# Graph attention in two layers: the fourth plain score behind the value matmuls, and three exponentials a step

## Chip, cores, metric

One core of a Trainium2 chip. The metric is device microseconds of one execution of the program, the median of several runs.

## What is computed

Two layers of masked multi-head attention on 4096 rows of 128 features, each followed by a feed-forward block. Cut to its core:

```python
qkv = layer_norm(x, g1, be1) @ w_qkv            # 8 heads of 16
scores = jnp.einsum('nhd,mhd->hnm', q, k) * SCALE
scores = jnp.where((adj != 0)[None], scores, -jnp.inf)
attn = jax.nn.softmax(scores, axis=-1)
out = jnp.einsum('hnm,mhd->nhd', attn, v).reshape(n, DIM)
x = x + out @ w_proj + b_proj
h2 = layer_norm(x, g2, be2)
x = x + jax.nn.gelu(h2 @ w1 + b1) @ w2 + b2
```

## The kernel before

A layer has three phases with barriers between them: the projections (`project`), the attention (`attend`), and the output projection with the feed-forward block. The change touches the attention alone, which takes most of the time.

The attention computes each score twice. Once plainly, with queries on the partitions (`score_a`, called A here), so that VectorE can take the masked maximum of each row (`take_max`, L802). And once transposed, with keys on the partitions and the maxima already subtracted by two more rows of the operands (`score_b`, called B), so that ScalarE's exponential of it (`exp_pair`, L667) can go straight into the value matmul (`gather_v`, L459, called V). There are 16 passes a layer (8 blocks of 512 queries, 4 heads at a time) of 32 steps, one for each tile of 128 keys; 512 steps a layer. The plain scores run ahead of the others by a pass and 20 scores (`FIRST`, 148): each step issues four of the plain scores for a later pass, A0 to A3, and the last 37 steps have none left.

Plain scores have three PSUM banks, used in turn: a score waits for the take of the one three before it (`a_done`). The B scores of a step have four banks, one a head, written again in each step as soon as their exponentials are done (`b_exped`). V has one bank that sums over the 32 steps of a pass. A take of A0 opens a new tile of the row mask and so waits for that tile as well as for the score; those of A1 to A3 wait for their score alone.

TensorE's matmuls for A, B and the masks have 48, 50 or 64 rows and stand in one half of the array's rows each, so that two neighbours on different halves can run at once (`r0` is 0 or 64). The four value matmuls use all rows and 32 columns each. The mask of the B scores is added on TensorE, as an identity matmul of bf16 in two halves (`add_mask`, L472, called m): for heads 0 and 1 in every step, and for heads 2 and 3 only in steps that are not `pooled`, which are the even steps in the even passes of layer 0 (called full-mask steps). In all others GpSimd multiplies the exponentials of heads 2 and 3 by a 0/1 mask (`mask_pair`, L950), in place, ahead of V. The second half of a bank's mask waits until the first halves of that pair are done (`half_added`), since both halves of the array write to one bank then.

V of a step is issued two steps later (`LAG`). `p_buf`, where the exponentials go, has four slots. ScalarE also makes row masks (L684), in about every other pass of layer 0, and keeps V's sums once a pass (L675). SyncE issues all DMAs of the phase in an order sorted by step numbers. At the end of a pass the maxima go to DRAM and come back as two rows of the query operand (`max_dram`, `q_ready`), for which the first B0 of a pass waits. Each engine otherwise follows the order in which its code is written.

In a step the order on TensorE is A0 A1, B0 B1, m m, B2 B3, m m, A2 A3, V; a full-mask step has two more pairs of m, around A2 A3. B0 waits for the first exponential of the step before, B2 for the second.

Of the kernel before, what the change touches and what calls it, by code (L numbers as in the profile page):

```python
# [57 lines left out]
def scores_before(t):  # L58
    return min(FIRST + 4 * t, NSC)
# [12 lines left out]
def gnn_kernel(nc, x, adj, adj_t, weights, signs, ident, ident_f, out):  # L72
    ctx = ExitStack()
    with ctx:
# [3 lines left out]
        def sem(name):  # L78
            return ctx.enter_context(nc.semaphore(name))
# [82 lines left out]
        max_ready, hi_ready, hi_kept, neg_ready = sem("max_ready"), sem("hi_ready"), sem("hi_kept"), sem("neg_ready")  # L162
        turned, max_stored, q_ready = sem("turned"), sem("max_stored"), sem("q_ready")
        half_added = sem("half_added")
        b_scored, b_exped, pv_done, o_kept = sem("b_scored"), sem("b_exped"), sem("pv_done"), sem("o_kept")
        o_stored = [sem("o_stored_0"), sem("o_stored_1")]

        o_loaded, o_turned, attn_ready = sem("o_loaded"), sem("o_turned"), sem("attn_ready")
# [44 lines left out]
        def masked_before(L, t):  # L213
            return sum(POOLED[l][STEPS] for l in range(L)) + POOLED[L][t]
# [14 lines left out]
        def _(sp):  # L229
# [51 lines left out]
            def load_added(L, i):  # L281
                nb, s = i // MT, i % MT
                if i >= 4:
                    sp.wait_ge(mt_loaded[i % 4], i // 4 * 16)
                if nb > 0:
                    sp.wait_ge(b_scored, L * 2 * STEPS + 2 * ((nb - 1) * 2 * MT + MT + s) + 2)
                sp.dma_start(mask_t[:, s, :], mt_dram[i]).then_inc(mt_loaded[i % 4], 16)

            def load_q(L, nb):
                if nb >= Q_SLOTS:  # L290
                    sp.wait_ge(b_scored, L * 2 * STEPS + (nb - Q_SLOTS + 1) * 4 * MT)
                slot = (L * NB + nb) % Q_SLOTS
                sp.dma_start(q_t[:, slot].rearrange("p i c -> p (i c)").bitcast(F32),
                             q_dram[nb].rearrange("p i c -> p (i c)")).then_inc(q_loaded[slot], 16)
# [108 lines left out]
        def _(pe):  # L403
# [43 lines left out]

            def gather_v(L, t):
                quad, s = t // MT % 2, t % MT
                pe.wait_ge(b_exped, L * 2 * STEPS + 2 * t + 2)  # L450
                if pooled(L, t):
                    pe.wait_ge(p_masked, masked_before(L, t + 1))
                if s == 0:
                    done = L * 2 * NB + t // MT
                    if done > 0:
                        pe.wait_ge(o_kept, done)
                for j in range(4):
                    h = 4 * quad + j
                    mm = pe.matmul(ps_o[32 * j:32 * j + 32, :], v_sb[:, (s * HEADS + h) * VW:(s * HEADS + h) * VW + 32],  # L459
                                   p_buf[:, t % P_SLOTS, j, :], start=s == 0, stop=s == MT - 1, skip_group_check=True)  # L460
                mm.then_inc(pv_done, 1)
# [13 lines left out]
            def b_step(L, t):  # L475


                nb, quad, s = t // (2 * MT), t // MT % 2, t % MT
                jobs = range(scores_before(t), scores_before(t + 1))
                for j in jobs[:2]:  # L480
                    score_a(L, j)
                if L == 0:
                    pe.wait_ge(t_made, nb * MT + s + 1)
                else:
                    pe.wait_ge(mt_loaded[s % 4], (nb * MT + s) // 4 * 16 + 16)
                if t > 0:
                    pe.wait_ge(b_exped, L * 2 * STEPS + 2 * t - 1)
                if s == 0:
                    pe.wait_ge(q_ready, (L * PASSES + t // MT + 1) * 64)
                score_b(L, t, 0), score_b(L, t, 1)  # L490
                if len(jobs) >= 4:
                    add_mask(s, 0, 0), add_mask(s, 1, 1).then_inc(half_added, 1)
                    added[0] += 1
                    if t > 0:
                        pe.wait_ge(b_exped, L * 2 * STEPS + 2 * t)
                    score_b(L, t, 2), score_b(L, t, 3)
                    pe.wait_ge(half_added, added[0])
                    if pooled(L, t):
                        add_mask(s, 1, 0), add_mask(s, 0, 1).then_inc(b_scored, 2)
                        for j in jobs[2:]:  # L500
                            score_a(L, j)
                    else:
                        add_mask(s, 1, 0), add_mask(s, 0, 1).then_inc(b_scored, 1)
                        add_mask(s, 2, 0), add_mask(s, 3, 1).then_inc(half_added, 1)
                        added[0] += 1
                        for j in jobs[2:]:
                            score_a(L, j)
                        pe.wait_ge(half_added, added[0])
                        add_mask(s, 3, 0), add_mask(s, 2, 1).then_inc(b_scored, 1)
                else:  # L510
                    for j in range(2):
                        mm = pe.matmul(ps_b[:, j, :], idb[:], mask_t[:, s, :], start=False, stop=True)
                    mm.then_inc(b_scored, 1)
                    for j in jobs[2:]:
                        score_a(L, j)
                    if t > 0:
                        pe.wait_ge(b_exped, L * 2 * STEPS + 2 * t)
                    score_b(L, t, 2)
                    mm = score_b(L, t, 3)
                    if not pooled(L, t):  # L520
                        for j in range(2, 4):
                            mm = pe.matmul(ps_b[:, j, :], idb[:], mask_t[:, s, :], start=False, stop=True)
                    mm.then_inc(b_scored, 1)
                if t >= LAG:
                    gather_v(L, t - LAG)

            def attend(L):
                for n in range(FIRST):
                    score_a(L, n)
                for t in range(STEPS):  # L530
                    b_step(L, t)
                for t in range(STEPS - LAG, STEPS):
                    gather_v(L, t)
# [86 lines left out]
        def _(act):  # L620
# [38 lines left out]
                    round_qk(gi)  # L659
                    keep_v(gi, g)  # L660

            def exp_pair(L, t, half):
                k = L * 2 * STEPS + 2 * t + half
                act.wait_ge(b_scored, k + 1)
                if half == 0 and t >= P_SLOTS:
                    act.wait_ge(pv_done, L * STEPS + t - P_SLOTS + 1)
                nc.scalar.activation(p_buf[:, t % P_SLOTS, 2 * half:2 * half + 2, :], ps_b[:, 2 * half:2 * half + 2, :],  # L667
                                     ACT.Exp, scale=SCALE).then_inc(b_exped, 1)

            def keep_o(L, i):  # L670
                gi = L * 2 * NB + i
# [15 lines left out]
            def attend(L):  # L687
                visits = [v for v in range(NV) if rows_made(L, v)]
                made = 0
                while made < len(visits) and visit_step(visits[made]) < 3:  # L690
                    mask_rows(visits[made])
                    made += 1
                for t in range(STEPS):
                    if t > LAG and t % MT == LAG:
                        keep_o(L, t // MT - 1)
                    exp_pair(L, t, 0)
                    exp_pair(L, t, 1)
                    while made < len(visits) and visit_step(visits[made]) - 3 < t + 1:
                        mask_rows(visits[made])
                        made += 1  # L700
                keep_o(L, 2 * NB - 1)
# [214 lines left out]
        def _(pool):  # L916
# [13 lines left out]
            def make_masks(t):  # L930
                nb, s, slot = t // (2 * MT), t % MT, t % M_SLOTS
                m = mask01[:, slot, :]
                pool.wait_ge(adjt_loaded[slot], fills(0, t) * 16)
                pool.tensor_scalar(m, m.bitcast(U32), 1.0, 0.0, ALU.min, ALU.max).then_inc(mask01_made, 1)  # L934
                if nb > 0:
                    pool.wait_ge(b_scored, 2 * (t - MT) + 2)
                    if s == 0:
                        pool.wait_ge(mt_stored, nb * MT * 16)
                pool.wait_ge(mask01_made, MADE[t + 1])
                pool.tensor_scalar(mask_t[:, s, :], m, -MASKED, MASKED, ALU.mult, ALU.add).then_inc(t_made, 1)  # L940

            def mask_pair(L, t):
                pool.wait_ge(b_exped, L * 2 * STEPS + 2 * t + 2)
                if made(L, t):
                    pool.wait_ge(mask01_made, MADE[t + 1])
                else:
                    pool.wait_ge(adjt_loaded[t % M_SLOTS], fills(L, t) * 16)  # L947
                p = p_buf[:, t % P_SLOTS, 2:4, :].bitcast(I32)
                m = mask01[:, t % M_SLOTS, :].rearrange("p (a c) -> p a c", a=1).broadcast_to([P, 2, TILE])
                pool.tensor_tensor(p, p, m, ALU.mult).then_inc(p_masked, 1)  # L950
# [70 lines left out]
```

## Time and profile before

| what | value |
|---|---|
| median of 3 runs | 3551.73 us (3551.18 to 3558.91) |
| the profiled execution | 3553.85 us, span 3552.1 us |
| TensorE busy | 3402.5 us, 96% |
| VectorE busy | 2847.8 us, 80% |
| GpSimd busy | 2482.2 us, 70% |
| ScalarE busy | 2334.7 us, 66% |

Shares are of the span. The attention of layer 0 lies from about 207 to 1685 us, that of layer 1 from about 1998 to 3437 us. The times of VectorE, GpSimd and ScalarE are those of their instructions; a matmul's end is modelled, and its time contains the flight through the array.

### The profile page before, as it was taken

Reading aid. Unit: us, or ns where it says so; the run is one execution under the profiler, and the core shown is the slowest. Engines: PE = TensorE matmul, PEld = TensorE weight load, DVE = VectorE, ACT = ScalarE, POOL = GpSimd, SP = SyncE. Lnnn points to the kernel's source line nnn. Section 1 sums busy time; section 2 is a strip of 40 time slices with the busy share of each in tenths; the row PEclk is TensorE's granted clock in tenths of the full one; section 3 lists DMA queues with packets and bytes.
Section 4 is the critical chain, followed back from the end, with each engine's and each line's share of the span. In section 5 each row is a group of like instructions: output and inputs, shape, how many; then the busy total and the mean of one; then the engine's idle time right before and its main releaser. Section 6 shows DMA issues by size and latency. Waiting matters only on the chain.

```text
span 3552.1 us, 68184 instructions
## 1 busy us (share of the span) xinstructions
PE 3402.5 (96%) x22292; PEld 1415.3 (40%) x22312; DVE 2847.8 (80%) x8964; ACT 2334.7 (66%) x2596; POOL 2482.2 (70%) x1476
## 2 busy tenths in 40 slices
PE   5999999999999999999768999999999999999988
PEld 3443333333333333332544433333333333333326
DVE  6898888888888888880458898999989999989604
ACT  4348777777778787868342366666666666666753
POOL 1057878787878788789110388888888888888870
PEclk9689999999999999999887699999999999999989
DMA  4578787878786978774222455555555555555432
GB/s 134 175 225 264 240 272 233 283 230 293 220 285 216 297 222 293 231 254 118 90 92 102 136 169 175 172 173 171 175 172 171 176 168 179 166 179 167 148 92 69
DMA packets 487006, 677.34 MB, mean 191 GB/s; under 512 B 57952, under 2 KB 279264, under 8 KB 482272
## 3 DMA queue, kind: packets, MB, share of 16 engines
q1 hardware_dynamic: 486224, 672.88, 60.7%
q8 instruction: 182, 2.98, 0.3%
q14 instruction: 168, 1.38, 0.1%
q10 hardware_dynamic: 432, 0.10, 0.0%
HBM read 508.67 MB, written 166.20 MB: 190 GB/s over the span
## 4 chain that ended last, share of the span: by engine, by line
PE 44%; POOL 38%; issue 11%; DMA 2%; ACT 1%; POOLq 1%; DVE 1%; SPq 1%; DVEq 0%; ACTq 0%
POOL arena L950 38%; PE PS L445 15%; PE PS L459 12%; PE PS L472 7%; PE PS L466 6%; PE PS L421 3%; POOLq L928 1%; DMA q_t<-max_dram 1%; ACT arena L667 1%; DVE arena L762 0%; PE PS L582 0%; PE PS L412 0%; SPq L303 0%; POOL arena L940 0%; POOLq L947 0%
## 5 line engine op out<-in xcount | busy, mean ns | idle before, releaser
L802 DVE CUSTOM_DVE_ANT_0 spill<-PS,mask_n 128x512 bf16<-128x512 f32 x4096 | 2594.9, 688 | 323.7 <-PE PS L445 315.1
L667 ACT ACTIVATE arena<-PS 128x1024 f32<-128x1024 f32 x2048 | 1986.4, 1022 | 812.0 <-PE PS L472 777.7
L950 POOL TENSOR_TENSOR arena<-arena,mask 128x1024 int32<-128x1024 int32 x896 | 2130.7, 2378 | 547.5 <-ACT arena L667 542.6
L445 PE MATMUL PS<-k_t,q_t 48*128 48x512 f32 x4096 | 1407.9, 539 | 15.9 <-DMA q_t<-q_dram 12.0
L459 PE MATMUL PS<-arena,v_sb 128*32 128x512 f32 x8192 | 1095.1, 607 | 6.4 <-POOL arena L950 5.6
L445 PEld LDWEIGHTS PS<-k_t,q_t 48*128 48x128 f32 x4096 | 619.6, 195 | 1049.0 <-DVE pmax L802 932.3
L466 PE MATMUL PS<-q_t,k_t 50*128 50x512 f32 x4096 | 909.6, 478 | 9.8 <-DMA q_t<-max_dram 9.0
L472 PE MATMUL PS<-arena,idb 64*128 64x512 bf16 x4304 | 836.0, 390 | 0.0
L466 PEld LDWEIGHTS PS<-q_t,k_t 50*128 50x128 f32 x4096 | 396.5, 187 | 109.9 <-issue 73.5
L472 PEld LDWEIGHTS PS<-arena,idb 64*128 64x128 bf16 x4304 | 208.3, 95 | 475.4 <-issue 291.2
L802 DVE DVE_READ_ACCUMULATOR2_ANT pmax<- 128x1 f32 x4096 | 344.6, 84 | 0.0
L459 PEld LDWEIGHTS PS<-arena,v_sb 128*32 128x32 f32 x8192 | 161.9, 108 | 260.5 <-issue 257.3
L934 POOL TENSOR_SCALAR mask<-mask 128x512 int32<-128x512 uint32 x256 | 157.2, 614 | 140.4 <-DMA mask<-in_adj_t 131.9
L923 POOL TENSOR_SCALAR arena<-arena 128x4 f32<-128x4 f32 x32 | 7.3, 228 | 322.4 <-DVE arena L753 322.4
L684 ACT ACTIVATE mask_n<-adj_in,far 128x512 bf16<-128x512 uint32 x256 | 184.8, 723 | 44.1 <-DVE pmax L802 31.0
L940 POOL TENSOR_SCALAR arena<-mask 128x512 bf16<-128x512 int32 x256 | 158.1, 618 | 37.5 <-POOL mask L934 34.3
L868 DVE RECIPROCAL arena<-PS 128x32 f32<-128x32 f32 x16 | 5.7, 357 | 206.2 <-PE PS L543 205.4
L421 PE MATMUL PS<-arena,wts 128*128 128x512 f32 x256 | 114.5, 601 | 0.0
L713 ACT ACTIVATE arena<-PS,wts 128x512 f32<-128x512 f32 x64 | 43.9, 687 | 52.6 <-PE PS L572 50.9
L629 ACT ACTIVATE arena<-PS,wts 128x512 f32<-128x512 f32 x32 | 24.9, 777 | 77.4 <-PE PS L412 45.6
L412 PE MATMUL PS<-idf,arena 128*128 128x128 f32 x64 | 12.3, 323 | 63.7 <-DVE arena L762 63.7
L421 PEld LDWEIGHTS PS<-arena,wts 128*128 128x128 f32 x256 | 48.5, 195 | 54.6 <-issue 54.6
(51 smaller groups left out, 841.7 us busy)
## 6 DMA issues: line engine op xcount, KB each, us to landing
mask<-m_dram SPq DMA_DIRECT2D x768, 256.0 KB, 2.8
mask_n<-mn_dram SPq DMA_DIRECT2D x768, 128.0 KB, 2.8
adj_in<-in_adj SPq DMA_DIRECT2D x256, 256.0 KB, 4.2
mask<-in_adj_t SPq DMA_DIRECT2D x256, 256.0 KB, 4.2
m_dram<-mask SPq DMA_DIRECT2D x256, 256.0 KB, 3.7
mn_dram<-mask_n SPq DMA_DIRECT2D x256, 128.0 KB, 4.3
mt_dram<-arena SPq DMA_DIRECT2D x256, 128.0 KB, 3.5
arena<-mt_dram SPq DMA_DIRECT2D x256, 128.0 KB, 2.9
```

Source lines behind the costliest of these rows:

```text
L421: pe.matmul(PS[:, 2 + i % 4, :], wts[:, C_QK + i * P:C_QK + (i + 1) * P], xn_t[:, gx % 2, :], start=True, stop=True).then_inc(qk_ready, 1)
L445: pe.matmul(ps_a[:, (L * NSC + n) % A_BANKS, :], q_t[r0:r0 + KROWS, gb % Q_SLOTS, pair, q * P:(q + 1) * P], k_t[r0:r0 + KROWS, pair, mb * ...
L459: mm = pe.matmul(ps_o[32 * j:32 * j + 32, :], v_sb[:, (s * HEADS + h) * VW:(s * HEADS + h) * VW + 32], p_buf[:, t % P_SLOTS, j, :], start= ...
L466: return pe.matmul(ps_b[:, j, :], k_t[r0:r0 + BROWS, pair, s * P:(s + 1) * P], q_t[r0:r0 + BROWS, (L * NB + nb) % Q_SLOTS, pair, :], start ...
L472: return pe.matmul(ps_b[:, j, :], idb[r0:r0 + 64, :], mask_t[r0:r0 + 64, s, :], start=False, stop=part != j % 2)
L667: nc.scalar.activation(p_buf[:, t % P_SLOTS, 2 * half:2 * half + 2, :], ps_b[:, 2 * half:2 * half + 2, :], ACT.Exp, scale=SCALE).then_inc( ...
L684: nc.scalar.activation(mask_n[:, slot, :], adj_in[:, m % ADJ_SLOTS, :].bitcast(U32), ACT.Exp, bias=far[:], scale=MASKED).then_inc(n_made, 1)
L713: nc.scalar.activation(g_t[:, f, :], PS[:, 4 + f, :], ACT.Gelu_apprx_tanh, bias=wts[:, C_B1 + f:C_B1 + f + 1]).then_inc(gelu_done, 1)
L802: dve.tensor_tensor_reduce(spill[:, bank, :], ps_a[:, bank, :], mask_n[:, v % N_SLOTS, :], 1.0, LOWEST, ALU.subtract, ALU.max, pmax[:, p % ...
L934: pool.tensor_scalar(m, m.bitcast(U32), 1.0, 0.0, ALU.min, ALU.max).then_inc(mask01_made, 1)
L940: pool.tensor_scalar(mask_t[:, s, :], m, -MASKED, MASKED, ALU.mult, ALU.add).then_inc(t_made, 1)
L950: pool.tensor_tensor(p, p, m, ALU.mult).then_inc(p_masked, 1)
```

## The change

On TensorE, A3 of a step is issued after V, beside A0 of the next step. A1 moves next to B2, B3 next to a mask piece, and A2 next to the last mask piece of the first pair. A common step is A3' A0, B0 B1, m m, B2 A1, m B3, A2 m, V, where A3' is the one carried over. A full-mask step is A3' A0, B0 B1, m m, B2 A1, m B3, m m, A2 m, m m, V.

On ScalarE the exponentials of heads 2 and 3, one instruction of 1024 columns before, are two of 512, each with its own semaphore in both directions (`scored`, `exped`). In common steps with plain scores head 2 goes first, then heads 0 and 1, then head 3; in all others heads 0 and 1 go first. B2 waits for the exponential of head 2, B3 for that of head 3. GpSimd waits for both. VectorE, SyncE and the DMAs keep their instructions and order; they wait for the new semaphores where they waited for the old ones.

```diff
             def b_step(L, t):
...
-                jobs = range(scores_before(t), scores_before(t + 1))
-                for j in jobs[:2]:
-                    score_a(L, j)
+                n, last = scores_before(t), scores_before(t + 1)
+                done = L * STEPS + t
+                if n > scores_before(t - 1):
+                    score_a(L, n - 1)
+                if last > n:
+                    score_a(L, n)
...
+                if t > 0:
+                    pe.wait_ge(exped[0], done)
                 score_b(L, t, 0), score_b(L, t, 1)
-                if len(jobs) >= 4:
+                if last > n:
                     add_mask(s, 0, 0), add_mask(s, 1, 1).then_inc(half_added, 1)
                     added[0] += 1
                     if t > 0:
-                        pe.wait_ge(b_exped, L * 2 * STEPS + 2 * t)
-                    score_b(L, t, 2), score_b(L, t, 3)
+                        pe.wait_ge(exped[1], done)
+                    mm = score_b(L, t, 2)
+                    if pooled(L, t):
+                        mm.then_inc(scored[1], 1)
+                    score_a(L, n + 1)
                     pe.wait_ge(half_added, added[0])
+                    add_mask(s, 1, 0)
+                    if t > 0:
+                        pe.wait_ge(exped[2], done)
+                    mm = score_b(L, t, 3)
                     if pooled(L, t):
-                        add_mask(s, 1, 0), add_mask(s, 0, 1).then_inc(b_scored, 2)
-                        for j in jobs[2:]:
-                            score_a(L, j)
+                        mm.then_inc(scored[2], 1)
+                        score_a(L, n + 2), add_mask(s, 0, 1).then_inc(scored[0], 1)
                     else:
-                        add_mask(s, 1, 0), add_mask(s, 0, 1).then_inc(b_scored, 1)
                         add_mask(s, 2, 0), add_mask(s, 3, 1).then_inc(half_added, 1)
                         added[0] += 1
-                        for j in jobs[2:]:
-                            score_a(L, j)
+                        score_a(L, n + 2), add_mask(s, 0, 1).then_inc(scored[0], 1)
                         pe.wait_ge(half_added, added[0])
-                        add_mask(s, 3, 0), add_mask(s, 2, 1).then_inc(b_scored, 1)
+                        add_mask(s, 3, 0).then_inc(scored[2], 1), add_mask(s, 2, 1).then_inc(scored[1], 1)
...
-            def exp_pair(L, t, half):
-                k = L * 2 * STEPS + 2 * t + half
-                act.wait_ge(b_scored, k + 1)
-                if half == 0 and t >= P_SLOTS:
+            def exp_heads(L, t, part):
+                act.wait_ge(scored[part], L * STEPS + t + 1)
+                if t >= P_SLOTS:
                     act.wait_ge(pv_done, L * STEPS + t - P_SLOTS + 1)
-                nc.scalar.activation(p_buf[:, t % P_SLOTS, 2 * half:2 * half + 2, :], ps_b[:, 2 * half:2 * half + 2, :],
-                                     ACT.Exp, scale=SCALE).then_inc(b_exped, 1)
+                heads = (slice(0, 2), slice(2, 3), slice(3, 4))[part]
+                nc.scalar.activation(p_buf[:, t % P_SLOTS, heads, :], ps_b[:, heads, :],
+                                     ACT.Exp, scale=SCALE).then_inc(exped[part], 1)
...
-                    exp_pair(L, t, 0)
-                    exp_pair(L, t, 1)
+                    for part in (1, 0, 2) if pooled(L, t) and scores_before(t + 1) > scores_before(t) else (0, 1, 2):
+                        exp_heads(L, t, part)
```

TensorE in a common step of layer 1, before: L459 is V, L445 a plain score, L466 a B score, L472 a half mask. The rows run from one V to the next.

```order
L459 MATMUL PS<-arena,v_sb 32x512 [waits p_masked,b_exped]
L459 MATMUL PS<-arena,v_sb 32x512 x3
L445 MATMUL PS<-k_t,q_t 128x512 [waits a_done] x2
L466 MATMUL PS<-q_t,k_t 128x512 [waits b_exped,mt_loaded_3]
L466 MATMUL PS<-q_t,k_t 128x512
L472 MATMUL PS<-arena,idb 128x512 x2
L466 MATMUL PS<-q_t,k_t 128x512 [waits b_exped]
L466 MATMUL PS<-q_t,k_t 128x512
L472 MATMUL PS<-arena,idb 128x512 [waits half_added]
L472 MATMUL PS<-arena,idb 128x512
L445 MATMUL PS<-k_t,q_t 128x512 [waits a_done] x2
```

The same step after the change: L466 is V there, L449 a plain score, L473 a B score, L479 a half mask.

```order
L466 MATMUL PS<-arena,v_sb 32x512 [waits p_masked,exped_01]
L466 MATMUL PS<-arena,v_sb 32x512 x3
L449 MATMUL PS<-k_t,q_t 128x512 [waits a_done] x2
L473 MATMUL PS<-q_t,k_t 128x512 [waits exped_01,mt_loaded_3]
L473 MATMUL PS<-q_t,k_t 128x512
L479 MATMUL PS<-arena,idb 128x512 x2
L473 MATMUL PS<-q_t,k_t 128x512 [waits exped_2]
L449 MATMUL PS<-k_t,q_t 128x512 [waits a_done]
L479 MATMUL PS<-arena,idb 128x512 [waits half_added]
L473 MATMUL PS<-q_t,k_t 128x512 [waits exped_3]
L449 MATMUL PS<-k_t,q_t 128x512 [waits a_done]
L479 MATMUL PS<-arena,idb 128x512
```

Two plain scores stand behind V in both, but they are A3' and A0 now; ahead of V a plain score and the last mask piece, which releases the first exponential pair, take the place of A2 A3.

ScalarE in common steps of layer 1, before (L667 is the exponential):

```order
L667 ACTIVATE arena<-PS 128x1024 [waits pv_done,b_scored]
L667 ACTIVATE arena<-PS 128x1024 [waits b_scored]
L667 ACTIVATE arena<-PS 128x1024 [waits pv_done,b_scored]
L667 ACTIVATE arena<-PS 128x1024 [waits b_scored]
L667 ACTIVATE arena<-PS 128x1024 [waits pv_done,b_scored]
```

And after (L682 is the exponential; `scored_2` stands for head 2, `scored_01` for heads 0 and 1):

```order
L682 ACTIVATE arena<-PS 128x512 [waits pv_done,scored_2]
L682 ACTIVATE arena<-PS 128x1024 [waits pv_done,scored_01]
L682 ACTIVATE arena<-PS 128x512 [waits pv_done,scored_3]
L682 ACTIVATE arena<-PS 128x512 [waits pv_done,scored_2]
L682 ACTIVATE arena<-PS 128x1024 [waits pv_done,scored_01]
```

One of two instructions a step became two of half its size, and one of these now stands ahead of the pair of heads 0 and 1.

## Rows read from the trace of the kernel before

**Rows 1.** The page: span, busy time of each engine, chain that ended last.

```profile
span 3552.1 us, 68184 instructions
PE 3402.5 (96%) x22292; PEld 1415.3 (40%) x22312; DVE 2847.8 (80%) x8964; ACT 2334.7 (66%) x2596; POOL 2482.2 (70%) x1476
...
PE 44%; POOL 38%; issue 11%; DMA 2%; ACT 1%; POOLq 1%; DVE 1%; SPq 1%; DVEq 0%; ACTq 0%
```

**Rows 2.** Windows, 100 us of layer 1: busy by engine, PEclk, DMA share, GB/s.

```profile
2500.00:2600.00 100.00, 100.00 (x712) 39.45 (x709) 90.32 (x290) 69.28 (x72) 84.36 (x36) 1.00 0.64 192
```

**Rows 3.** Timeline, layer 1: start, length in us, engine, line, operation, [idle before].

```profile
2499.33 0.69 DVE L802 CUSTOM_DVE_ANT_0 spill<-PS,mask_n 128x512 bf16<-128x512 f32 x1 [0.29 <-PE PS L445]
...
2499.72 0.39 PE L472 MATMUL PS<-arena,idb 64*128 64x512 bf16 x2
...
2500.09 0.18 PEld L445 LDWEIGHTS PS<-k_t,q_t 48*128 48x128 f32 x1 [0.17 <-DVE pmax L802]
2500.15 1.94 ACT L667 ACTIVATE arena<-PS 128x1024 f32<-128x1024 f32 x2 [0.86 <-PE PS L472]
...
2500.52 1.06 PE L459 MATMUL PS<-arena,v_sb 128*32 128x512 f32 x8
...
2501.51 0.50 PE L445 MATMUL PS<-k_t,q_t 48*128 48x512 f32 x2
...
2501.86 0.40 PE L466 MATMUL PS<-q_t,k_t 50*128 50x512 f32 x2
...
2502.09 0.39 PE L472 MATMUL PS<-arena,idb 64*128 64x512 bf16 x2
...
2502.14 0.58 PE L466 MATMUL PS<-q_t,k_t 50*128 50x512 f32 x2
2502.16 0.69 DVE L802 CUSTOM_DVE_ANT_0 spill<-PS,mask_n 128x512 bf16<-128x512 f32 x1 [0.29 <-PE PS L445]
2502.17 2.38 POOL L950 TENSOR_TENSOR arena<-arena,mask 128x1024 int32<-128x1024 int32 x1 [0.42 <-ACT arena L667]
...
2502.57 0.39 PE L472 MATMUL PS<-arena,idb 64*128 64x512 bf16 x2
```

**Rows 4.** Waits in the same 100 us: total, times, longest.

```profile
PEld PS L445 <- DVE pmax L802: 31.2, 46, 0.8
```

**Rows 5.** Timeline of a full-mask step in layer 0.

```profile
1001.82 0.50 PE L445 MATMUL PS<-k_t,q_t 48*128 48x512 f32 x2
...
1002.86 0.61 PE L472 MATMUL PS<-arena,idb 64*128 64x512 bf16 x4
...
1003.55 0.39 PE L472 MATMUL PS<-arena,idb 64*128 64x512 bf16 x2
...
1003.74 0.69 DVE L802 CUSTOM_DVE_ANT_0 spill<-PS,mask_n 128x512 bf16<-128x512 f32 x1
...
1003.87 1.07 PE L459 MATMUL PS<-arena,v_sb 128*32 128x512 f32 x8
...
1004.87 0.50 PE L445 MATMUL PS<-k_t,q_t 48*128 48x512 f32 x2
```

**Rows 6.** The same step, a window that ends ahead of A3.

```profile
1003.12 0.58 PE L445 MATMUL PS<-k_t,q_t 48*128 48x512 f32 x1
```

**Rows 7.** Groups of instructions on ScalarE: busy us, mean ns, idle before.

```profile
L667 ACT ACTIVATE arena<-PS 128x1024 f32<-128x1024 f32 x2048 | 1986.4, 1022 | 812.0 <-PE PS L472 777.7 <-PE PS L512 34.2
L684 ACT ACTIVATE mask_n<-adj_in,far 128x512 bf16<-128x512 uint32 x256 | 184.8, 723 | 44.1 <-DVE pmax L802 31.0 <-DMA adj_in<-in_adj 13.2
...
L675 ACT COPY o_sb<-PS 128x512 f32<-128x512 f32 x32 | 18.9, 591 | 8.3 <-PE PS L459 8.3
```

**Rows 8.** The page's groups: the half-mask matmuls.

```profile
L472 PE MATMUL PS<-arena,idb 64*128 64x512 bf16 x4304 | 836.0, 390 | 0.0
```

**Rows 9.** Timeline of TensorE behind a pass edge in layer 0.

```profile
301.89 0.50 PE L466 MATMUL PS<-q_t,k_t 50*128 50x512 f32 x2 [1.59 <-DMA q_t<-max_dram]
...
302.69 0.41 PE L472 MATMUL PS<-arena,idb 64*128 64x512 bf16 x2
```

**Rows 10.** Timeline in the last steps of layer 0, without plain scores.

```profile
1619.98 7.17 POOL L950 TENSOR_TENSOR arena<-arena,mask 128x1024 int32<-128x1024 int32 x3
```

More of the change, by code:

```diff
@@ L164, in gnn_kernel @@
         half_added = sem("half_added")
-        b_scored, b_exped, pv_done, o_kept = sem("b_scored"), sem("b_exped"), sem("pv_done"), sem("o_kept")
+        scored = [sem("scored_01"), sem("scored_2"), sem("scored_3")]
+        exped = [sem("exped_01"), sem("exped_2"), sem("exped_3")]
+        pv_done, o_kept = sem("pv_done"), sem("o_kept")
         o_stored = [sem("o_stored_0"), sem("o_stored_1")]
@@ L285, in load_added @@
                 if nb > 0:
-                    sp.wait_ge(b_scored, L * 2 * STEPS + 2 * ((nb - 1) * 2 * MT + MT + s) + 2)
+                    sp.wait_ge(scored[0], L * STEPS + (nb - 1) * 2 * MT + MT + s + 1)
                 sp.dma_start(mask_t[:, s, :], mt_dram[i]).then_inc(mt_loaded[i % 4], 16)
@@ L290, in load_q @@
                 if nb >= Q_SLOTS:
-                    sp.wait_ge(b_scored, L * 2 * STEPS + (nb - Q_SLOTS + 1) * 4 * MT)
+                    for part in range(3):
+                        sp.wait_ge(scored[part], L * STEPS + (nb - Q_SLOTS + 1) * 2 * MT)
                 slot = (L * NB + nb) % Q_SLOTS
@@ L449, in gather_v @@
                 quad, s = t // MT % 2, t % MT
-                pe.wait_ge(b_exped, L * 2 * STEPS + 2 * t + 2)
+                pe.wait_ge(exped[0], L * STEPS + t + 1)
                 if pooled(L, t):
                     pe.wait_ge(p_masked, masked_before(L, t + 1))
+                else:
+                    pe.wait_ge(exped[1], L * STEPS + t + 1)
+                    pe.wait_ge(exped[2], L * STEPS + t + 1)
                 if s == 0:
@@ L485, in b_step @@
                     pe.wait_ge(mt_loaded[s % 4], (nb * MT + s) // 4 * 16 + 16)
-                if t > 0:
-                    pe.wait_ge(b_exped, L * 2 * STEPS + 2 * t - 1)
                 if s == 0:
                     pe.wait_ge(q_ready, (L * PASSES + t // MT + 1) * 64)
+                if t > 0:
+                    pe.wait_ge(exped[0], done)
                 score_b(L, t, 0), score_b(L, t, 1)
-                if len(jobs) >= 4:
+                if last > n:
                     add_mask(s, 0, 0), add_mask(s, 1, 1).then_inc(half_added, 1)
@@ L512, in b_step @@
                         mm = pe.matmul(ps_b[:, j, :], idb[:], mask_t[:, s, :], start=False, stop=True)
-                    mm.then_inc(b_scored, 1)
-                    for j in jobs[2:]:
-                        score_a(L, j)
+                    mm.then_inc(scored[0], 1)
                     if t > 0:
[L517 to L520, printed above, removed]
+                        pe.wait_ge(exped[1], done)
+                        pe.wait_ge(exped[2], done)
+                    if pooled(L, t):
+                        score_b(L, t, 2).then_inc(scored[1], 1), score_b(L, t, 3).then_inc(scored[2], 1)
+                    else:
+                        score_b(L, t, 2), score_b(L, t, 3)
                         for j in range(2, 4):
                             mm = pe.matmul(ps_b[:, j, :], idb[:], mask_t[:, s, :], start=False, stop=True)
-                    mm.then_inc(b_scored, 1)
+                            mm.then_inc(scored[j - 1], 1)
                 if t >= LAG:
@@ L527, in attend @@
             def attend(L):
-                for n in range(FIRST):
+                for n in range(0, FIRST - 1):
                     score_a(L, n)
@@ L935, in make_masks @@
                 if nb > 0:
-                    pool.wait_ge(b_scored, 2 * (t - MT) + 2)
+                    pool.wait_ge(scored[0], t - MT + 1)
                     if s == 0:
@@ L942, in mask_pair @@
             def mask_pair(L, t):
-                pool.wait_ge(b_exped, L * 2 * STEPS + 2 * t + 2)
+                pool.wait_ge(exped[1], L * STEPS + t + 1)
+                pool.wait_ge(exped[2], L * STEPS + t + 1)
                 if made(L, t):
```

## The prediction

> **What bounds the kernel now.** The page first: TensorE is busy 96% of a span of 3552.1 us, VectorE 80%, GpSimd 70%, ScalarE 66%, and the chain that ended last runs through PE and POOL [rows 1]. A 96% that contains waits with a matmul still in flight decides nothing, so I read one stretch of layer 1, where every step is alike: the granted clock is 1.00 there (2.4 GHz), and 36 mask products in 100 us make a step some 2.8 us [rows 2]. Then the timeline of one step [rows 3], to see which waits repeat. Call the four plain scores of a step A0 to A3, the four scores for the softmax B0 to B3, the half-mask matmuls m, and the four value matmuls V. VectorE starts its take of A0 at 2499.33 and again at 2502.16: a step is 2.83 us. Follow it round:
> - A0 and A1 start at 2501.51; A0 takes 0.50 and ends at 2502.01; VectorE starts on it at 2502.16. That is 0.65 us, and VectorE had been idle for 0.29 before it.
> - Three banks hold plain scores, so A3 needs A0's bank. From VectorE's start at 2499.33 to the weight load of A3 at 2500.09, whose wait the row puts down to that engine: 0.76.
> - A3 to V: 2500.09 to 2500.52, 0.43. V to the next A0: 2500.52 to 2501.51, 0.99 (the stretch 0.995 that repeats).
>
> 0.65 + 0.76 + 0.43 + 0.99 = 2.83. **This loop through the three banks is the bound** of such a step. The grouped waits agree: the weight loads of plain scores are the ones on PE that wait for VectorE, 31.2 us in 100, most of it while V runs [rows 4]. A second loop is just as long by eye: m ends at 2500.11, the two exponentials run from 2500.15 for 1.94 to 2502.09, and B2 starts at 2502.14. But m had started only at 2502.09 and its 0.21 of columns was under way, so B2 lost little by it.
>
> A step that adds all its masks on PE (every second one in the even passes of layer 0) goes from A0 at 1001.82 to A0 at 1004.87, 3.05 us [rows 5]. Its A3 does not hold up V, since two more mask slots follow; the matmuls themselves bound it. In the last 37 steps of a layer, without plain scores, three mask products follow each other in 7.17 us: 2.39 a step, GpSimd's own rate [rows 10].
>
> **How many of each.** Each layer has 475 steps with plain scores. 4304 half-mask matmuls [rows 8] = 4 x 950 + 4 x 126, so 126 of the 950 are such full-mask steps and 824 are not.
>
> **The change part by part.**
>
> *The number of matmuls and slots* stays: six pairs and V in a common step, eight pairs and V in a full-mask step. A3 of a step now starts after V, beside the next A0; A2 is the last one ahead of V. A2 needs the bank of that A3. So the loop has the same four members: first score behind V, its take, last score ahead of V, V. Carrying the score over does not by itself lengthen the distance, and I give it nothing.
>
> *What it does change in the loop* is which take comes first behind V. Before, it is that of A0, the one that opens a new mask tile and waits for two semaphores, the tile's and the score's. Its start lies 0.15 behind the matmul's end (2502.01 to 2502.16, rows 3). A take that waits for one is to be seen in the full-mask step: A2 starts at 1003.12 and takes 0.58 [rows 6], so it ends at 1003.70, and VectorE, idle by then, starts at 1003.74 [rows 5], 0.04 later. After the change the first take behind V is A3's, with one wait; A0's second wait falls behind a take that is still running. Worth 0.11 us: 0.54 + 0.76 + 0.43 + 0.99 = **2.72**. Bounds of this term: 0 (the delay belongs to the spot behind V, not to the waits) and 0.11.
>
> *Split exponentials.* Two of 1024 columns a step become one of 1024 and two of 512. One of 1024 takes 1.02; a copy of 512 out of PSUM takes 0.59, the exponential of 512 from SBUF 0.72 [rows 7]. Two in a row start 0.92 apart (1.94 less 1.02). I take 0.59 and 0.49 for the distance, by the copy, since it reads the same memory; the upper end is 0.62. ScalarE's load goes from 1.84 to 0.92 + 2 x 0.49 = 1.90, with the row masks of the odd passes 2.53: under 2.72, so free, and 2.8 at the upper ends. What matters is the order. The first pair's last mask piece now stands behind A2's wait, and its exponential is needed by B0, the second slot behind V. That loop: B0 to the mask piece that waits for half_added, 301.89 to 302.69, 0.80 [rows 9]; B3, issued behind that wait, shows its weight load, 0.10 (a score behind V takes 0.50, one whose load is hidden 0.40, rows 3); one slot 0.24 (2501.86 to 2502.09); the last piece 0.39; to ScalarE 0.04; 1.02; to B0 0.05, or 0.16 since B0 waits for two semaphores. Sum **2.64 to 2.75**. This is what is late next, within 0.03 of the other loop on either side. I take 2.72 to 2.73 for a common step, a gain of **0.10**: 824 x 0.10 = -82 us. Bounds: -91 (0.11) and -41 (0.05).
>
> B2's wait for both exponentials goes: it now needs the one that was done first. As said, it cost little. GpSimd needs the last exponential, which ends some 1.6 behind V instead of 1.57; its 2.38 still fits in 2.72, and V takes its product two steps later.
>
> *Full-mask steps.* B3 stands behind the half_added wait with an unhidden f32 load, 0.10, where a bf16 piece stood, whose load costs next to nothing. The piece behind it on its row half, m31, is late by this, the pair that waits for it too (1002.86 to 1003.55 to 1003.87 in rows 5), and nothing here has slack. +0.10 x 126 = **+13 us**; bounds 0 and +20.
>
> *Pass edges.* The maxima of a pass are complete about half a microsecond later (the last take stands behind V), and the softmax scores of the first step wait for them by way of DMA: 1.59 once [rows 9]. The extra reductions also meet less idle time on VectorE. 30 edges at 0.1: **+3**; bounds 0 and +10.
>
> *The tail* (37 steps a layer) stays at GpSimd's 2.39: its scores and exponentials keep their order, and 1.90 of ScalarE fits. SP's queue and all DMAs are the same; they are issued by steps, so they only come 3% closer together.
>
> **Sum.** -82 + 13 + 3 = -66. The profiled execution took 3553.9 us, so 3488; the median of the runs stands 2.1 lower, 3551.7, so **3486 us**.
>
> **Rivals.**
> 1. *The exponential's loop takes over (slower).* The first pair's scores are signalled behind A2's wait, and everything down to B0 is in series. If the 512-column exponentials follow at 0.62, the first one (head 2) delays the 1024 one by some 0.05, and with B0's double wait 0.05 dearer than my 0.16 the loop is 2.75 + 0.10 = 2.85. From 2.81 on it eats the whole gain. 824 x 0.03 + 13 + 3 = +41: some **3592**, and 3550 where it only equals the old bound. For it: the two loops are within 0.03 already. Against: every piece but two has its own row. Chance 0.14.
> 2. *Nothing in the loop moves.* The 0.15 belongs to waking VectorE behind V. Then 2.83 stays and the full-mask steps pay: 3552 + 16 = **3568**. Against it are the rows of the one-wait take. Chance 0.07.
> 3. *Unlike pairs do not overlap.* All pairs in the trace are of one type. PE's own time for a common step, with no wait, is 0.99 (V) + 0.34 (A to B) + 0.24 (B to m) + 0.48 (m to m, rows 3) + 0.24 + 0.32 (m to V, rows 5) = 2.61. If an f32 score and a bf16 mask piece run one after the other, two slots of 512 columns at 2.4 GHz come on top, 0.43: 3.04, or 0.21 more than 2.83; a full-mask step gets 0.43 + 0.11: 824 x 0.21 + 126 x 0.54 = +241, **3793**. For it: nothing shows such a pair. Against: the halves have separate rows, loads and banks. Chance 0.09.
> 4. *Semaphore updates.* A common step has nine matmuls that update one, before it had seven, and each is a little work at PE's end. No row isolates it; the nearest is that A to B takes 0.34 behind two updates and B to m 0.24 behind none, so up to 0.05 each: 2.72 + 0.10 at most, 2.77 in the middle, **3530**. Chance 0.05. The Trainium skill ("TensorE: Matmul & The Clock Gate", Part 3, the cost per tile) says that increments of packed matmuls serialise at 26.3 ns each; by that figure the sum would be some 43 us higher, an estimate, and no row here confirms it.
>
> The forecast's own mechanism has 0.65, with 3461 to 3531 by its bounds.
>
> **Range and chances.** 3455 to 3568 takes in the forecast (0.65), rival 4 (0.05), rival 2 (0.07) and the milder part of rival 1 (0.06). A measurement tells about 0.2% (7 us) from no change. Faster 0.74, same 0.07, slower 0.19.
>
> **What would show it.** In layer 1, V to V at 2.71 to 2.75; VectorE's first take behind V 0.04 behind the matmul's end; its idle time before a take down from 0.29 to about 0.2. The full-mask steps at 3.15. ScalarE's 512-column exponentials at 0.59. The forecast is wrong if PE's waits name ScalarE at B0 for most steps (rival 1), if the first take still starts 0.15 late (rival 2), or if the slot with B3 and a mask piece takes 0.45 instead of 0.24 (rival 3).

## The result, and the profile after

| | before | after |
|---|---|---|
| median | 3553.03 us (4 runs, 3551.18 to 3558.91) | 3503.24 us (4 runs, 3495.38 to 3505.25) |
| profiled execution | 3553.85, span 3552.1 | 3504.94, span 3503.2 |

The ratio is 0.9853, with a 95% interval of 0.9833 to 0.9873: **1.5% faster**, 50 us, where 3486 had been forecast.

The page after, to be read beside [rows 1]. TensorE's share is the same 96%, ScalarE has gained 145 us of work, and the chain that ended last has left GpSimd (38% of it before, 1% now).

```profile
span 3503.2 us, 71453 instructions
PE 3351.8 (96%) x22292; PEld 1483.3 (42%) x22312; DVE 2840.6 (81%) x8964; ACT 2479.3 (71%) x3620; POOL 2484.2 (71%) x1476
...
PE 80%; issue 5%; DVE 3%; DMA 2%; POOL 1%; SPq 1%; ACT 1%; POOLq 1%; DVEq 0%; ACTq 0%
```

Where the time went is best read from the distance between the first value matmuls of successive steps, taken from both traces:

| steps (how many) | median, before | median, after | sum, before | sum, after | change |
|---|---|---|---|---|---|
| layer 1, common (472) | 2.820 | 2.734 | 1336.7 | 1294.5 | -42.1 |
| layer 0, odd passes (224) | 2.820 | 2.734 | 650.2 | 630.8 | -19.4 |
| layer 0, even passes, common (124) | 2.820 | 2.712 | 351.7 | 340.3 | -11.4 |
| layer 0, full-mask (124) | 3.050 | 3.212 | 380.2 | 397.9 | +17.7 |
| last steps of both layers (78) | 2.39 | 2.39 | 186.8 | 187.5 | +0.7 |
| all that lies ahead, between and behind | | | 646.6 | 652.1 | +5.6 |

The sum of the changes, -48.9, is the difference of the spans. The last row is nearly all code that the change doesn't touch. It varies between the traces of this study as well, from 646.1 to 652.5 (646.9 in experiment 1 below and 651.8 in experiment 4, both without a carried score), and its cause stays open.

A common step of layer 1 after the change. L449 is a plain score, L473 a B score, L479 a half mask, L466 V. A piece mjk is the half mask of head j on half k of the array's rows: m10 waits for half_added and m01 is the last one of the first pair. These rows answer to [rows 3]; start and length are in us.

```profile
2499.93 0.21 PEld L473 LDWEIGHTS PS<-q_t,k_t 50*128 50x128 f32 x2
...
2500.20 0.69 DVE L817 CUSTOM_DVE_ANT_0 spill<-PS,mask_n 128x512 bf16<-128x512 f32 x1 [0.19 <-PE PS L449]
...
2500.28 0.41 PE L479 MATMUL PS<-arena,idb 64*128 64x512 bf16 x2
...
2500.76 0.39 PE L479 MATMUL PS<-arena,idb 64*128 64x512 bf16 x1
2500.77 0.49 PE L473 MATMUL PS<-q_t,k_t 50*128 50x512 f32 x1
...
2500.93 2.11 ACT L682 ACTIVATE arena<-PS 128x512 f32<-128x512 f32 x3 [0.63 <-PE PS L473]
2500.95 0.18 PEld L449 LDWEIGHTS PS<-k_t,q_t 48*128 48x128 f32 x1
...
2501.11 0.39 PE L479 MATMUL PS<-arena,idb 64*128 64x512 bf16 x1
...
2501.42 1.06 PE L466 MATMUL PS<-arena,v_sb 128*32 128x512 f32 x8
...
2501.53 1.02 ACT L682 ACTIVATE arena<-PS 128x1024 f32<-128x1024 f32 x1
...
2502.42 0.50 PE L449 MATMUL PS<-k_t,q_t 48*128 48x512 f32 x2
...
2502.67 0.21 PEld L473 LDWEIGHTS PS<-q_t,k_t 50*128 50x128 f32 x2
2502.75 0.45 PE L473 MATMUL PS<-q_t,k_t 50*128 50x512 f32 x2
2502.95 0.69 DVE L817 CUSTOM_DVE_ANT_0 spill<-PS,mask_n 128x512 bf16<-128x512 f32 x1 [0.22 <-PE PS L449]
```

(The row at 2500.93 merges the three exponentials of a step; the one at 2501.53 is the middle one, of heads 0 and 1, from a narrower view. The row at 2499.93, B0's and B1's weight loads, is from a narrower view too.)

The first scores behind V end at 2502.92 and VectorE starts at 2502.95, 0.03 later; before it was 0.15. The rest of the loop through the banks: take to A2's weight load 0.75 (2500.20 to 2500.95), A2 to V 0.47, V to the next scores 1.00. Note the 0.47, which was 0.43: V now waits for the mask piece at 2501.11, not for A2. I put that piece's lateness down to B3's weight load, which stands in the open at 2500.76 behind the wait for half_added: it is 0.34 from B3 to the piece that follows on the same half of the array. Experiment 6 tests this. B0 and B1 are late as well: the exponential of heads 0 and 1 ended at 2502.55 and their weight loads start at 2502.67, 0.25 behind A's start where it was 0.11 (2501.62 in the trace before). The masks behind them come 0.59 to 0.62 behind A, before 0.58.

The loop through that exponential can be followed in these rows from one weight load of B0 (2499.93) to the next (2502.67): 0.83 to m10, 0.35 to m01, 0.39 for it, 0.04 to ScalarE, 1.02 for the exponential, 0.11 to B0's load. That is 2.73 to 2.74, the median step.

A full-mask step after, to be read beside [rows 5]:

```profile
788.35 0.50 PE L449 MATMUL PS<-k_t,q_t 48*128 48x512 f32 x2
...
788.97 0.41 PE L479 MATMUL PS<-arena,idb 64*128 64x512 bf16 x2
...
789.45 0.39 PE L479 MATMUL PS<-arena,idb 64*128 64x512 bf16 x1
789.46 0.49 PE L473 MATMUL PS<-q_t,k_t 50*128 50x512 f32 x1
789.67 0.38 PE L479 MATMUL PS<-arena,idb 64*128 64x512 bf16 x1
...
789.80 0.84 PE L479 MATMUL PS<-arena,idb 64*128 64x512 bf16 x4
```

From B3's pair to the piece m31 on B3's half it is 789.45 to 789.80, 0.35; before, the two pairs of pieces at this place followed each other at 0.23. And the first masks stand 0.62 behind A. Two delays, then, where I had counted one.

### The profile page after: what moved, and what is told of

The parts are those of the page before. It is cut to its first block, busy times and chain, and to the rows that moved or that the text cites. A ratio compares the mean times of both kernels' runs of the same rounds, so it can differ in the third digit from the quotient of the medians.

```text
span 3503.2 us, 71453 instructions
## 1 busy us (share of the span) xinstructions
PE 3351.8 (96%) x22292; PEld 1483.3 (42%) x22312; DVE 2840.6 (81%) x8964; ACT 2479.3 (71%) x3620; POOL 2484.2 (71%) x1476
## 4 chain that ended last, share of the span: by engine, by line
PE 80%; issue 5%; DVE 3%; DMA 2%; POOL 1%; SPq 1%; ACT 1%; POOLq 1%; DVEq 0%; ACTq 0%
PE PS L466 28%; PE PS L449 18%; PE PS L473 16%; PE PS L479 14%; DVE spill L817 2%; PE PS L425 2%; PE PS L527 1%; POOL arena L966 1%; ACT arena L682 1%; DMA q_t<-max_dram 1%; POOLq L943 1%; PE PS L597 0%; DMA max_dram<-stage_t 0%; SPq L307 0%; DVE arena L777 0%
## 5 line engine op out<-in xcount | busy, mean ns | idle before, releaser
L682 ACT ACTIVATE arena<-PS 128x512 f32<-128x512 f32 (+1 forms) x3072 | 2133.3, 739 | 615.3 <-PE PS L473 371.6
L449 PE MATMUL PS<-k_t,q_t 48*128 48x512 f32 x4096 | 1694.2, 542 | 14.2 <-DMA q_t<-q_dram 12.1
L473 PE MATMUL PS<-q_t,k_t 50*128 50x512 f32 x4096 | 1258.1, 485 | 11.8 <-DMA q_t<-max_dram 9.0
L479 PE MATMUL PS<-arena,idb 64*128 64x512 bf16 x4304 | 1150.5, 389 | 0.0
L466 PE MATMUL PS<-arena,v_sb 128*32 128x512 f32 x8192 | 1094.8, 606 | 8.2 <-POOL arena L966 7.9
L449 PEld LDWEIGHTS PS<-k_t,q_t 48*128 48x128 f32 x4096 | 627.3, 195 | 942.4 <-DVE pmax L817 898.6
L473 PEld LDWEIGHTS PS<-q_t,k_t 50*128 50x128 f32 x4096 | 594.5, 188 | 209.1 <-issue 112.1
L479 PEld LDWEIGHTS PS<-arena,idb 64*128 64x128 bf16 x4304 | 310.4, 94 | 376.5 <-PE PS L479 230.7
L466 PEld LDWEIGHTS PS<-arena,v_sb 128*32 128x32 f32 x8192 | 161.7, 108 | 248.2 <-issue 248.2
```

What stands on the lines that cost most here:

```text
L449: pe.matmul(ps_a[:, (L * NSC + n) % A_BANKS, :], q_t[r0:r0 + KROWS, gb % Q_SLOTS, pair, q * P:(q + 1) * P], k_t[r0:r0 + KROWS, pair, mb * ...
L473: return pe.matmul(ps_b[:, j, :], k_t[r0:r0 + BROWS, pair, s * P:(s + 1) * P], q_t[r0:r0 + BROWS, (L * NB + nb) % Q_SLOTS, pair, :], start ...
L479: return pe.matmul(ps_b[:, j, :], idb[r0:r0 + 64, :], mask_t[r0:r0 + 64, s, :], start=False, stop=part != j % 2)
L682: nc.scalar.activation(p_buf[:, t % P_SLOTS, heads, :], ps_b[:, heads, :], ACT.Exp, scale=SCALE).then_inc(exped[part], 1)
```

## The experiments

All kernels below compute the whole result. Lengths of a common step are medians in layer 1, from V to V. The kernel before was run again beside each group: 3551.7 us beside the first four, 3554.7 beside the second four, and the ratios are to these.

**1. The kernel before, with one wait moved.** The row-mask tile of the next four takes is waited for at A3's take.

```diff
-                if i == 0:
-                    if rows_made(L, v):
-                        dve.wait_ge(n_made, ROWS_MADE[v + 1])
+                if n == 0 or (i == 3 and v + 1 < NV):
+                    u = v if n == 0 else v + 1
+                    if rows_made(L, u):
+                        dve.wait_ge(n_made, ROWS_MADE[u + 1])
                     else:
-                        dve.wait_ge(mn_loaded[v % N_SLOTS], rows_loads(L, v) * 16)
+                        dve.wait_ge(mn_loaded[u % N_SLOTS], rows_loads(L, u) * 16)
```

> The kernel before, with one edit on VectorE: the wait for the next row-mask tile stands at the take of A3 (which finds a backlog) and no longer at the take of A0, so the first take behind V waits for the score alone. Order and waits of TensorE, ScalarE and GpSimd are those of before. Theory (the double wait of the first take behind V costs 0.11 us in the loop through the three banks): a common step goes from 2.82 to between 2.71 and 2.76, the latter where the loop through both exponentials takes over (0.39 + 0.04 + 1.94 + 0.05 + 0.34 = 2.76); 824 steps x 0.06 to 0.11 = 50 to 90 us, so 3463 to 3503 beside 3553. Full-mask steps stay at 3.05. Rival (the delay belongs to the place behind V): 3553, and VectorE still starts 0.15 behind the matmul's end.

Measured: 3506.93 us, ratio 0.9872 (0.9858 to 0.9887). A common step takes 2.770, in the even passes of layer 0 2.712, a full-mask step 3.10. The timeline of layer 1:

```profile
2540.11 1.94 ACT L667 ACTIVATE arena<-PS 128x1024 f32<-128x1024 f32 x2 [0.83 <-PE PS L472]
...
2541.22 0.50 PE L445 MATMUL PS<-k_t,q_t 48*128 48x512 f32 x2
...
2541.76 0.69 DVE L803 CUSTOM_DVE_ANT_0 spill<-PS,mask_n 128x512 bf16<-128x512 f32 x1
...
2542.11 0.19 PEld L466 LDWEIGHTS PS<-q_t,k_t 50*128 50x128 f32 x2 [0.22 <-ACT arena L667]
```

A0 ends at 2541.72 and VectorE starts at 2541.76. The wait, not the place, was the 0.11. And the next bound shows at once: B2's load waits for ScalarE now, which [rows 3] had shown without cost. So one moved wait on VectorE brings nearly as much as the whole change (45 us against 50). It stops at 2.77 because both exponentials lie in a loop of that length, 0.39 + 0.04 + 1.94 + 0.05 + 0.34 = 2.76. The full-mask steps did not stay at 3.05 as I had expected: B2's load waits for the exponentials of the step before there as well (608.65 to 608.70 in layer 0 of its trace).

**2. The changed kernel, with the same edit.** There it puts two waits on the first take behind V.

> The changed kernel with the same edit on VectorE: the wait for the next row-mask tile moves to the take of A3, which is there the first one behind V, so that one has two waits again. Theory: its start goes from 0.04 to 0.15 behind the matmul's end and a common step from 2.73 to 2.84; 824 x 0.11 = +90, some 3590; about 3560 to 3600, slower than before, since the full-mask steps keep their 3.21. Rival (the place decides): 3503, no change.

Measured: 3566.86 us, ratio 1.0037 (1.0023 to 1.0052): slower than before. A common step is back at 2.820, and the full-mask steps keep 3.211.

```profile
2540.69 0.49 PE L449 MATMUL PS<-k_t,q_t 48*128 48x512 f32 x2
...
2541.33 0.69 DVE L818 CUSTOM_DVE_ANT_0 spill<-PS,mask_n 128x512 bf16<-128x512 f32 x1 [0.28 <-PE PS L449]
```

2541.18 to 2541.33 is the 0.15 again. The step is 2.82 and not the 2.84 I expected, since with VectorE late the last mask piece no longer holds up V. With experiment 1 this shows the cause of the gain from both sides: the change without its side effect on the waits costs 15 us.

**3. The split exponentials alone**, with TensorE's order of before.

```diff
-                    exp_pair(L, t, 0)
-                    exp_pair(L, t, 1)
+                    for part in (0, 1, 2):
+                        exp_heads(L, t, part)
```

(with B2 waiting for `exped[1]`, B3 for `exped[2]`, and the scores signalled apart, as in the change)

> TensorE's order of before (A2 and A3 ahead of V), with the changed kernel's three exponentials a step and their separate semaphores, heads 0 and 1 first, then head 2, then head 3. B2 waits for the exponential of head 2, B3 for that of head 3. Theory: the loop through the banks stays at 2.82 and the full-mask steps at 3.05, so nothing moves: 3553 within 7 us. Rival (the exponentials' loop was the real bound, and the split is what brought the gain): a common step at 2.73 or below, 3480 or below.

Measured: 3551.33 us, ratio 1.0000 (0.9990 to 1.0009), a common step of 2.820. As expected, but the next run shows that it proves less than I thought.

**4. The split, and the moved wait of experiment 1.**

> As the run with the split alone, and in addition the wait for the next row-mask tile at the take of A3, so that the first take behind V (A0) waits for one semaphore. No score is carried over V. Theory: both loops are relieved, the one through the banks is at 2.71 to 2.72 and the one through the exponentials well below; full-mask steps stay at 3.05: 3553 - 824 x 0.105 = 3466 (3460 to 3475), so faster than the changed kernel by some 35 us. If the carried score is needed for the gain, this one stays near 3553; if pairing unlike matmuls brings something of its own, it stays above 3503.

Measured: 3548.72 us, ratio 0.9991 (0.9981 to 1.0000). **Wrong by 83 us**: with the split on top of experiment 1 its gain is gone. The trace says why:

```profile
2540.26 2.00 ACT L682 ACTIVATE arena<-PS 128x1024 f32<-128x1024 f32 x3 [0.82 <-PE PS L479]
...
2542.32 0.18 PEld L473 LDWEIGHTS PS<-q_t,k_t 50*128 50x128 f32 x1 [0.16 <-ACT arena L682]
...
2542.41 0.09 PEld L479 LDWEIGHTS PS<-arena,idb 64*128 64x128 bf16 x1
...
2542.66 0.39 PE L479 MATMUL PS<-arena,idb 64*128 64x512 bf16 x1
...
2543.09 1.02 ACT L682 ACTIVATE arena<-PS 128x1024 f32<-128x1024 f32 x1 [0.82 <-PE PS L479]
```

Three exponentials in a row take 2.00, the pair took 1.94. B3 waits for the last of them, loads its weights in the open, and the mask piece on its half (2542.66) releases the next three. From 2540.26 to 2543.09 the loop is 2.83. This loop was there in experiment 3 as well (2.82 in its trace), next to the banks' loop of the same length, so that run could not tell them apart.

**5. The same, with head 2 first.**

```diff
-                    for part in (0, 1, 2):
+                    for part in (1, 0, 2) if pooled(L, t) and scores_before(t + 1) > scores_before(t) else (0, 1, 2):
```

> TensorE's order of before, three exponentials a step, the first take behind V with one wait, as the run that stayed at 3549, but with head 2's exponential ahead of that of heads 0 and 1, as in the changed kernel. Theory: in that run the loop m01, three exponentials in a row, B3 took over (0.39 + 0.04 + 0.92 + 0.48 + 0.60 + 0.05 + 0.34 = 2.82); with head 2 first only two of them lie in the loop and the banks' 2.71 is the bound again, full-mask steps near 3.05: 3553 - 824 x 0.105 = 3466 (3460 to 3480), faster than the changed kernel, without a carried score. If it stays near 3549, the cause of that run was another one (the number of waits on B2 and B3, or the unhidden load of B3 by itself).

Measured: **3464.62 us**, ratio 0.9748 (0.9728 to 0.9768). A common step takes 2.712, a full-mask step 3.043. The timeline of layer 1 on ScalarE, which works on head 2 while the last mask pieces are still being added:

```profile
2539.76 2.00 ACT L682 ACTIVATE arena<-PS 128x512 f32<-128x512 f32 x3 [0.71 <-PE PS L473]
2542.47 1.51 ACT L682 ACTIVATE arena<-PS 128x512 f32<-128x512 f32 x2 [0.70 <-PE PS L473]
```

Order alone is worth 84 us here. This kernel has the change's exponentials and the single wait, but carries no score over V, and it beats the changed kernel by 39 us. Summed as in the table above, its trace is 42.6 us shorter: 19 lie in the full-mask steps, which the carried order lengthens, 17 in the common steps of all passes, and 6 in the last row, which has no cause here.

**6. The changed kernel, with B3 ahead of the wait for half_added.**

```diff
-                    pe.wait_ge(half_added, added[0])
-                    add_mask(s, 1, 0)
                     if t > 0:
                         pe.wait_ge(exped[2], done)
                     mm = score_b(L, t, 3)
+                    pe.wait_ge(half_added, added[0])
+                    add_mask(s, 1, 0)
```

> The changed kernel with B3 issued ahead of the wait for half_added and of the mask piece m10, so that its weight load runs beside the plain score A1. Theory (the unhidden load of B3 costs 0.10 in the full-mask steps and lies in the loop through heads 0 and 1's exponential): full-mask steps from 3.21 to 3.11, common steps of whole passes from 2.735 to the banks' 2.71: 126 x 0.10 + 698 x 0.02 = -27, so 3476 (3470 to 3485). Rival (unlike pairs run one after the other, and that is where the 0.10 is): full-mask steps stay at 3.21, 3503.

Measured: 3474.17 us, ratio 0.9769 (0.9752 to 0.9787). Common steps 2.700, full-mask steps 3.130.

```profile
2542.26 0.39 PE L479 MATMUL PS<-arena,idb 64*128 64x512 bf16 x1
2542.27 0.39 PE L473 MATMUL PS<-q_t,k_t 50*128 50x512 f32 x1
2542.43 0.49 PE L449 MATMUL PS<-k_t,q_t 48*128 48x512 f32 x1
2542.50 0.39 PE L479 MATMUL PS<-arena,idb 64*128 64x512 bf16 x1
```

B3 and the mask piece start together, and the next piece on B3's half follows 0.23 later, the same as for a pair of one type. So the unlike matmuls do overlap, and the delay between B3 and the next piece was B3's weight load.

**7. The changed kernel, with heads 2 and 3 in one exponential again.**

```diff
+                if part == 1:
+                    act.wait_ge(scored[2], L * STEPS + t + 1)
...
-                heads = (slice(0, 2), slice(2, 3), slice(3, 4))[part]
+                heads = (slice(0, 2), slice(2, 4))[part]
...
-                    for part in (1, 0, 2) if pooled(L, t) and scores_before(t + 1) > scores_before(t) else (0, 1, 2):
+                    for part in (0, 1):
```

(B3 waits for the same exponential as B2)

> The changed kernel with the exponentials of heads 2 and 3 in one instruction of 1024 columns again, behind that of heads 0 and 1, as before. The carried score and TensorE's order stay. Theory (the score carried over V puts the last mask piece late, so the exponentials must be split and reordered for it to pay): the loop m01, two exponentials, B2, m10, B3, m01 takes 0.39 + 0.04 + 1.94 + 0.05 + 0.34 + 0.34 = 3.1 in a common step: 3553 + 824 x 0.28 + 20 = some 3800 (3750 to 3850). Rival (the split is free dressing): 3503.

Measured: 3725.28 us, ratio 1.0478 (1.0462 to 1.0495), a common step of 3.026. With heads 2 and 3 in one exponential behind that of heads 0 and 1, the carried score loses 222 us against the changed kernel. This edit takes back the split and the order together; one exponential of heads 2 and 3 ahead of that of heads 0 and 1 was not run, so it stays open which of the two the carried score needs. I had the loop 0.07 too long: half_added has long been reached when B2's wait ends, so B3's weight load is hidden.

```profile
2542.70 0.50 PE L474 MATMUL PS<-q_t,k_t 50*128 50x512 f32 x1
...
2543.04 0.39 PE L480 MATMUL PS<-arena,idb 64*128 64x512 bf16 x1
2543.05 0.40 PE L474 MATMUL PS<-q_t,k_t 50*128 50x512 f32 x1
...
2543.29 0.39 PE L480 MATMUL PS<-arena,idb 64*128 64x512 bf16 x1
```

B2 to m10 is 0.34, m10 to the last piece 0.25.

**8. The changed kernel, with one wait on B0.** The wait for the mask tile moves to the score behind V.

```diff
+                if L == 0:
+                    pe.wait_ge(t_made, nb * MT + s + 1)
+                else:
+                    pe.wait_ge(mt_loaded[s % 4], (nb * MT + s) // 4 * 16 + 16)
                 if n > scores_before(t - 1):
                     score_a(L, n - 1)
```

(and is removed from its place ahead of B0)

> The changed kernel with TensorE's wait for the mask tile moved from B0 to the score behind V (A3', which waits there anyway while V runs), so that B0 waits for the exponential alone. Theory (the loop through heads 0 and 1's exponential, 2.735, lies just over the banks' 2.71, with B0's two waits in it): common steps of whole passes go to 2.71, 698 x 0.02 = -15, so 3488, full-mask steps at 3.17 to 3.21. Rival (the banks' loop alone is the bound, 2.735 is its length): 3503, no change.

Measured: 3483.76 us, ratio 0.9796 (0.9781 to 0.9811). Common steps 2.713, full-mask steps 3.139. B0's load of this trace:

```profile
2540.92 1.03 ACT L682 ACTIVATE arena<-PS 128x1024 f32<-128x1024 f32 x1
...
2542.00 0.19 PEld L473 LDWEIGHTS PS<-q_t,k_t 50*128 50x128 f32 x2
```

It starts 0.05 behind the end of the exponential (2541.95), where it was 0.11 in the changed kernel. So a second wait on an instruction that others wait for costs on TensorE as well, 0.06 here, and the loop through heads 0 and 1's exponential was the bound of the changed kernel's common steps in layer 1 and the odd passes.

## Why the prediction was right, and where it was off

- **The bound before: confirmed.** The loop through the three banks held the step at 2.82. Taking 0.11 from one of its members (experiment 1) shortened every common step, and giving it back (experiment 2) undid the change's gain.
- **The double wait of the first take: confirmed, with its size.** Where VectorE is idle, the median from the matmul's end to its start is 0.15 with two waits (the kernel before, experiments 2 and 3) and 0.04 with one (the other seven kernels). In layer 1 the mask tile had landed 17 us earlier (median), so the take was not waiting for it. That the carried score itself brings nothing is confirmed too, and it costs more than the 13 and 3 us that I gave it: a kernel without it, with the same exponentials and the single wait, is 39 us faster (experiment 5).
- **"B2's wait for both exponentials cost little": right for the kernel before, and incomplete.** With the banks' loop at 2.71 the loop through both exponentials is the bound, at 2.77 (experiment 1). I had seen that the two loops were alike, and took nothing from it.
- **The loop through heads 0 and 1's exponential, 2.64 to 2.75, against the banks' 2.72: the term that was mis-sized.** It measured 2.73. I took a gain of 0.10 a step. In the even passes it was 0.108, in all others 0.086: there this loop, at 2.734, is the bound, with B0's second wait and B3's open load in it, as experiments 8 and 6 show by removing one each. The length after was forecast to 0.01 (2.72 to 2.73); the rest of the shortfall lies in the length before, for which I had taken 2.83 from one step where the median is 2.820. Over the 820 common steps of the table that is -73 instead of the -79 of steps and pass edges together.
- **Full-mask steps: mis-sized.** I gave them +0.10 for B3's load, and the step lost 0.16. Experiment 6 gives back 0.08 of it, experiment 8 0.07. The missing part is the late B0: I had checked the exponential's loop for the common steps and not for the ones that follow them, though B0 of a full-mask step waits for the exponential of a common one. +17.7 instead of +13.
- **Pass edges and the tail** fell within their bounds: the first two steps of a pass lie 17 us in all above the medians before and 19 after, and the tail is +0.7. The forecast's own upper end, 3531, had left out the +10 for the edges. The last row of the table, +5.6, was in no term.
- **The miss in all:** 17 us of a forecast gain of 66. About 6 are the common steps with the edges, 5 the full-mask steps, 1 the tail and 6 the last row of the table, whose cause is open.
- **The signs named beforehand:** V to V 2.73 in layer 1, the first take 0.03 to 0.04 behind the matmul, VectorE idle for 0.20 before it, and 0.596 for an exponential of 512 columns all came as forecast. The full-mask steps did not, at 3.21 instead of 3.15.
- **The rivals.** Rival 2 fell with experiments 1 and 2, rival 3 with experiment 6. Rival 1 was half right: the loop it names took over, but 0.08 below the point from which it would have cost. Rival 4 has no room left in this loop: experiment 5's common step has the same nine updates and takes 2.712, and the sum of the loop's members without them is 2.72. The Trainium skill ("TensorE: Matmul & The Clock Gate", Part 3) gives 26.3 ns for each increment. By that figure two more of them would make a step 0.05 longer, an estimate, and this did not show.

## What to carry to other kernels

Follow one repeating step round its loops and write down every loop within a few per cent of the bound, with its members: four of them lay between 2.71 and 2.83 us in the kernels here (through the banks, the exponential of heads 0 and 1, the two of a step, the three of a step), and each edit only paid down to the next. In such a loop it matters how many semaphores the waiting instruction names; a wait that is always early belongs on an instruction that finds a backlog. And where a matmul stands behind a wait that is still running, its weight load does too (0.10 us of the changed kernel's loop).

## What the runs showed that I had not expected

- A wait for a second semaphore costs an idle VectorE 0.11 us even when that semaphore was reached long before. Where the engine is busy it costs next to nothing: a take behind a running one starts 0.61 to 0.62 after it, with one wait or two. One wait, moved, was worth 45 us of 3552.
- Splitting an exponential of 1024 columns into two of 512 costs 0.06 us in a row of them (2.00 against 1.94), but in a loop it is the order that decides: 3549 with heads 0 and 1 first, 3465 with head 2 first.
- An f32 matmul and a bf16 one on different halves of the array run beside each other as two of one type do: 0.23 us a pair.
